# Four placements in a graph-attention kernel: inverse sums in PSUM, the last pair's order, a weight turned in row halves, count scatters among the mask's

## The reference

```python
q2 = (q @ wiq.T + biq).reshape(N, H, D).transpose(1, 0, 2)     # 16 heads of 64; k2, v2 alike
scores = jnp.einsum('hnd,hmd->hnm', q2, k2) * scale + mask[None]
attn = jax.nn.softmax(scores, axis=-1)
out = jnp.einsum('hnm,hmd->hnd', attn, v2)
out = out.transpose(1, 0, 2).reshape(N, OUT_F)
return out @ wo.T + bo
...
mask = mask.at[src, dst].set(w[edge_type - 1])     # 384 x 384, from 6144 edges
...
cnt = jax.ops.segment_sum(mask, dst, num_segments=n)     # next layer: edges per relation and target
out = out + mean @ weight[r]
```

## Time and profile before

| | us |
|---|---|
| median of 3 runs | 934.96 |
| lowest, highest run | 934.83, 941.38 |
| profiled execution | 936.0 |
| its span | 934.2 |
| TensorE busy in it | 909.6 |
| VectorE, GpSimd, ScalarE busy | 609.6, 488.5, 360.5 |

### The profile page before, as it was taken

One profiled execution on the slowest core, in us unless ns is written; L12 is line 12 of the kernel. 1 busy time (PEld: TensorE's weight loads), 2 busy tenths in 40 slices (PEclk: granted clock), 3 DMA queues, 4 the chain that ended last, 5 costly groups with the idle time before them and its releaser, 6 DMA issues.

```text
span 934.2 us, 13614 instructions
## 1 busy us (share of the span) xinstructions
PE 909.6 (97%) x4723; PEld 802.0 (86%) x4723; DVE 609.6 (65%) x1003; ACT 360.5 (39%) x568; POOL 488.5 (52%) x436
## 2 busy tenths in 40 slices
PE   4999999999999999999999999999999999999998
PEld 4999999998888887888888888888888888887886
DVE  6998888896996735655556565665656665434645
ACT  6433333344885334232323232223324345233532
POOL 5334443456686455757566575757685601320363
PEclk8999999999999999999999999999999999999999
DMA  8998755571336617454434435344333434332412
GB/s 207 239 279 224 226 159 153 152 198 1 53 52 198 166 16 269 114 155 108 154 103 159 149 112 167 94 149 113 96 107 127 158 124 139 118 105 90 137 44 91
DMA packets 89908, 128.60 MB, mean 138 GB/s; under 512 B 34481, under 2 KB 67457, under 8 KB 89857
## 3 DMA queue, kind: packets, MB, share of 16 engines
q1 hardware_dynamic: 72784, 123.54, 43.4%
q0 software_dynamic: 15552, 0.11, 4.1%
q10 hardware_dynamic: 1520, 4.30, 1.3%
HBM read 117.17 MB, written 7.59 MB: 134 GB/s over the span
## 4 chain that ended last, share of the span: by engine, by line
PE 89%; DVE 4%; ACT 2%; POOL 2%; DMA 1%; issue 1%; ACTq 0%; POOLq 0%; DVEq 0%
PE ps L671 48%; PE ps L471 17%; PE ps L745 8%; PE ps L515 4%; PE ps L634 4%; PE ps L595 2%; PE ps L551 2%; PE ps L538 1%; DMA weight_d<-weight_sum,cell 1%; PE ps L432 1%; PE ps L459 1%; DVE wlo_all L1372 1%; POOL weight_d L1865 1%; POOL mean_lo L1844 1%; PE ps L880 1%
## 5 line engine op out<-in xcount | busy, mean ns | idle before, releaser
L1372 DVE TENSOR_TENSOR wlo_all<-raw,whi_all 128x1024 fp32r<-128x1024 f32 x120 | 193.8, 1624 | 120.8 <-ACT whi_all L959 120.7
L471 PE MATMUL ps<-acts,whi_all 128*128 128x384 f32 (+1 forms) x640 | 164.2, 338 | 0.1
L1844 POOL TENSOR_TENSOR mean_lo<-mean_f,mean_hi 128x384 fp32r<-128x384 f32 x76 | 88.0, 1158 | 122.3 <-ACT mean_hi L1110 122.3
L1110 ACT ACTIVATE mean_hi<-mean_f 128x384 fp32r<-128x384 f32 x76 | 40.0, 526 | 272.7 <-DVE mean_f L1541 272.7
L671 PE MATMUL ps<-whi_all,mean_hi 128*128 128x512 f32 x452 | 139.8, 391 | 1.7 <-POOL mean_lo L1844 1.7
L671 PE MATMUL ps<-wlo_all,mean_hi 128*128 128x512 f32 x452 | 139.4, 390 | 0.0
L671 PE MATMUL ps<-whi_all,mean_lo 128*128 128x512 f32 x452 | 139.4, 390 | 0.0
L959 ACT ACTIVATE whi_all<-raw 128x1024 fp32r<-128x1024 f32 x120 | 124.6, 1049 | 23.7 <-PE ps L671 18.2
L471 PEld LDWEIGHTS ps<-acts,whi_all 128*128 128x128 f32 x640 | 116.7, 190 | 0.5 <-DVE acts L1384 0.4
L1865 POOL DMA_INDIRECT weight_d<-weight_sum,cell x48 | 95.6, 1991 | 27.6 <-DMA weight_d<-weight_sum,cell 16.7
L471 PE MATMUL ps<-acts,wlo_all 128*128 128x384 f32 (+1 forms) x320 | 107.8, 337 | 0.0
(11 more groups left out here) (209 smaller groups left out, 1723.7 us busy)
## 6 DMA issues: line engine op xcount, KB each, us to landing
raw<-in_L_gnn_weight SPq DMA_DIRECT2D x64, 512.0 KB, 3.3
rows_b<-rows_d SPq DMA_DIRECT2D x24, 384.0 KB, 5.3
raw<-in_L_gnn_w_gate SPq DMA_DIRECT2D x16, 512.0 KB, 3.3
raw<-in_L_gnn_W_self SPq DMA_DIRECT2D x16, 512.0 KB, 3.4
raw<-in_L_gnn_W_neigh SPq DMA_DIRECT2D x16, 512.0 KB, 3.8
count_d<-total_r SPq DMA_DIRECT2D x8, 576.0 KB, 5.5
rel_r<-count_d SPq DMA_DIRECT2D x8, 576.0 KB, 4.5
raw<-in_L_gnn_wq SPq DMA_DIRECT2D x32, 128.0 KB, 6.3
```

The costliest lines, as they stand in the source:

```text
L471: mm = pe.matmul(ps[:, j % 2, 0:N], stationary[j % RING][:, k, :], acts[:, a, moving, k, :], start=i == 0, stop=i == 3 * KT - 1)
L1110: act.activation(mean_of(q, k, 0)[:, 0, :], sums_of(q, k), ACT.Copy).then_inc(S["mean_hi"], 1)
L1372: dve.tensor_tensor(wlo_row[slot], raw[slot][:, :], whi_row[slot].bitcast(F32), ALU.subtract)\
L1844: pool.tensor_tensor(mean_of(q, k, 1)[:, 0, :], sums_of(q, k), mean_of(q, k, 0)[:, 0, :].bitcast(F32), ALU.subtract).then_inc(S["mean_lo"], 1)
```

## The change

Nothing is computed otherwise. Six edits:

1. `invert_sums` writes the reciprocals of heads 2 to 15 to columns 384 and on of PSUM bank 7, which `spread_sums` leaves unused, and copies them from there. It waits for `spread_read` before, and `read_spread` moves, on ScalarE, from the end of a pair to before `probs_high(o, 0)`.
2. The last pair of heads is written out on its own on TensorE, and its order on ScalarE and VectorE is changed with it; `make_pair(6)` moves behind `probs_low(o, 0)`.
3. `turn_output` turns row halves: 16 transposes of 64 rows into 64 columns each, one half in each bank; `column_high` and `column_low` read the new layout.
4. The last 16 mask scatters go in groups between the first 16 count scatters; `PAIR_AFTER` is eight counts later.
5. The 16 `meet` of the value units are spread otherwise, none in the last; the first two inversions come after the first two `probs_low`.
6. `sum_planes(0)` goes ahead of `row_parts(0)`, with a wait for `w_used`.

```diff
--- before.py
+++ after.py
@@ -196,6 +196,7 @@
         V_UNITS = NT * KT // 2
         V_COLS = 2 * P
         V_BANK = (0, 1, 6, 7)
+        ROWS = P // 2
         WO_BANK = (0, 2, 0, 2, 4, 6, 4, 6)
         T_ROOT = 7 * KT
         T_REL = T_ROOT + KT
@@ -209,7 +210,8 @@
         W_CREDIT = RING
         O_CREDIT = 2
         S_CREDIT = 2
-        PAIR_AFTER = (17, 19, 21, 25, 27, 29)
+        PAIR_AFTER = (25, 27, 29, 33, 35, 37)
+        MASK_ALONE = 2 * EC // 3
 
         FIRST = KT // 2
         TURNS = NT + KT - FIRST
@@ -456,8 +458,10 @@
                 if j > 5:
                     pe.wait_ge(S["w_lo"], T_WO + j - 1)
                 for k in range(KT):
-                    mm = pe.transpose(ps[:, WO_BANK[j] + k // 4, P * (k % 4):P * (k % 4) + P],
-                                      raw[j % RING][:, P * k:P * k + P], ident[:, :])
+                    for f in range(2):
+                        rows = slice(ROWS * f, ROWS * f + ROWS)
+                        mm = pe.transpose(ps[:, WO_BANK[j] + f, ROWS * k:ROWS * k + ROWS],
+                                          raw[j % RING][rows, P * k:P * k + P], ident[rows, rows])
                 mm.then_inc(S["weight_turned"], 1)
 
             def column_tile(g, j, a, ready=None):
@@ -601,27 +605,33 @@
                 e, o = 2 * pair, 2 * pair + 1
                 if pair and o + 1 < H:
                     scores(pair + 1, 0)
-                if o + 1 < H:
-                    scores(pair + 1, 1)
-                else:
-                    turn_output(0)
-                    turn_output(1)
+                if o + 1 == H:
+                    break
+                scores(pair + 1, 1)
                 if pair:
                     turn_probs(e, 0)
                     turn_probs(e, 1)
                     weigh_values(e - 1)
                 turn_probs(e, 2)
                 spread_sums(pair)
-                if o + 1 < H:
-                    scores(pair + 1, 2)
-                else:
-                    turn_output(2)
+                scores(pair + 1, 2)
                 turn_probs(o, 0)
                 turn_probs(o, 1)
-                if o + 1 == H:
-                    turn_output(3)
                 weigh_values(e)
                 turn_probs(o, 2)
+            turn_output(0)
+            turn_probs(H - 2, 0)
+            turn_probs(H - 2, 1)
+            spread_sums(H // 2 - 1)
+            turn_output(1)
+            weigh_values(H - 3)
+            turn_probs(H - 2, 2)
+            turn_probs(H - 1, 0)
+            turn_output(2)
+            turn_output(3)
+            turn_probs(H - 1, 1)
+            turn_probs(H - 1, 2)
+            weigh_values(H - 2)
             weigh_values(H - 1)
 
             def output_blocks(f, nt, blocks):
@@ -948,8 +958,9 @@
                 if j < RING:
                     act.wait_ge(S["w_used"], T_WO + (j + 1))
                 b = WO_BANK[j]
-                act.activation(whi[j][:, :, :] if j < RING else wo_t[0][:, j - RING, :, :],
-                               ps[:, b:b + 2, :].rearrange("p b (k n) -> p (b k) n", n=P), ACT.Copy)\
+                target = whi[j] if j < RING else wo_t[0][:, j - RING, :, :]
+                act.activation(target.rearrange("p k (f n) -> p k f n", f=2),
+                               ps[:, b:b + 2, :].rearrange("p f (k n) -> p k f n", n=ROWS), ACT.Copy)\
                    .then_inc(S["w_hi"], 1)
 
             def row_high(t, slot, use, used=None):
@@ -1057,26 +1068,27 @@
                     exp(o + 2, 0)
                 if not more:
                     column_high(0)
+                    column_high(1)
                 probs_high(e, 2)
                 if more:
                     exp(e + 2, 1)
                     exp(o + 2, 1)
-                else:
-                    column_high(1)
+                if more:
+                    read_spread(pair)
                 probs_high(o, 0)
                 if more:
                     exp(e + 2, 2)
                 else:
+                    read_spread(pair)
                     column_high(2)
                 probs_high(o, 1)
                 if more:
                     exp(o + 2, 2)
-                else:
+                probs_high(o, 2)
+                if not more:
                     column_high(3)
-                probs_high(o, 2)
                 if pair:
                     pair_high(pair - 1)
-                read_spread(pair)
 
             act.wait_ge(S["probs_turned"], H * NT)
             act.dma_start(xres[:, :, :], x.rearrange("(t p) d -> p t d", p=P)).then_inc(S["x_in"], 16)
@@ -1328,8 +1340,10 @@
                 dve.wait_ge(S["w_hi"], T_WO + (j + 1))
                 b = WO_BANK[j]
                 hi, lo = (whi[j], wlo[j]) if j < RING else [w[:, j - RING, :, :] for w in wo_t]
-                dve.tensor_tensor(lo[:, :, :], ps[:, b:b + 2, :].rearrange("p b (k n) -> p (b k) n", n=P),
-                                  hi[:, :, :].bitcast(F32), ALU.subtract).then_inc(S["w_lo"], 1)
+                dve.tensor_tensor(lo.rearrange("p k (f n) -> p k f n", f=2),
+                                  ps[:, b:b + 2, :].rearrange("p f (k n) -> p k f n", n=ROWS),
+                                  hi.rearrange("p k (f n) -> p k f n", f=2).bitcast(F32), ALU.subtract)\
+                   .then_inc(S["w_lo"], 1)
 
 
             def start_low(n):
@@ -1409,9 +1423,15 @@
             def invert_sums(o):
                 d0 = DH * (o % 2)
                 dve.wait_ge(S["exp_ready"], 6 * (o // 2) + 5 + o % 2)
-                link(dve.reciprocal(rinv[:, o % 2, :], rsum[:, o % 4, :]))
+                if o < 2:
+                    inverse = rinv[:, o, :]
+                else:
+
+                    dve.wait_ge(S["spread_read"], o // 2)
+                    inverse = ps[:, 7, N + NT * (o % 2):N + NT * (o % 2) + NT]
+                link(dve.reciprocal(inverse, rsum[:, o % 4, :]))
                 dve.tensor_copy(rinv_cols[:, o // 2 % 2, :, d0:d0 + DH],
-                                rinv[:, o % 2, :].unsqueeze(2).to_broadcast([P, NT, DH])).then_inc(S["sum_inverted"], 1)
+                                inverse.unsqueeze(2).to_broadcast([P, NT, DH])).then_inc(S["sum_inverted"], 1)
 
             def value_tiles(g):
                 met_now = g * KT * 2
@@ -1428,17 +1448,17 @@
                     if 6 <= n < 6 + NT:
                         score_max(0, n - 6)
                         score_max(1, n - 6)
-                    for n_met in range((1, 1, 2)[n % NT]):
+                    for n_met in range((2, 1, 1, 2, 1, 1, 2, 1, 1, 2, 2, 0)[n]):
                         meet(met_now)
                         met_now += 1
                     if n == V_UNITS - 2:
                         dve.wait_ge(S["w_lo"], g * KT + KT)
                         score_max(2, 0)
                         score_max(3, 0)
+                probs_low(0, 0)
+                probs_low(0, 1)
                 invert_sums(0)
                 invert_sums(1)
-                probs_low(0, 0)
-                probs_low(0, 1)
 
             for g in range(5):
                 eight_tiles(g, g + 1 if g < 3 else g - 3)
@@ -1466,25 +1486,24 @@
                     probs_low(e, 1)
                 if not more:
                     column_low(0)
-                if pair:
+                    column_low(1)
+                if pair and more:
                     make_pair(pair - 1)
                 probs_low(e, 2)
                 if more:
                     score_max(e + 2, 2)
                     score_max(o + 2, 2)
-                else:
-                    column_low(1)
                 probs_low(o, 0)
                 if more:
                     invert_sums(e + 2)
                 else:
+                    make_pair(pair - 1)
                     column_low(2)
                 probs_low(o, 1)
                 if more:
                     invert_sums(o + 2)
-                else:
-                    column_low(3)
                 probs_low(o, 2)
+            column_low(3)
 
             def last_pair_low(pair):
                 dve.wait_ge(S["pair_hi"], pair + 1)
@@ -1819,8 +1838,9 @@
 
             cells(0, 0, 0)
             pool.wait_ge(S["mask_based"], 16)
-            for c in range(EC):
+            for c in range(MASK_ALONE):
                 scatter_mask(c)
+
             def pair_low(pair):
                 pool.wait_ge(S["pair_hi"], pair + 1)
                 link(pool.tensor_tensor(o_f[:, pair, :], o_f[:, pair, :], acts[:, 0, 0, pair, :].bitcast(F32),
@@ -1829,6 +1849,9 @@
                                    None, ALU.add).then_inc(S["pair_lo"], 1)
 
             for c in range(EC):
+                if c % GROUP == 0:
+                    for m in range(MASK_ALONE + c, min(MASK_ALONE + c + GROUP, EC)):
+                        scatter_mask(m)
                 add_counts(c)
                 if c in PAIR_AFTER:
                     pair_low(PAIR_AFTER.index(c))
@@ -1874,9 +1897,10 @@
```

(5 more changed lines are left out.)

## The result

| | before | after |
|---|---|---|
| median of 8 executions each, side by side, us | 935.06 | 929.1 |
| time against before, 95% interval | | 0.9939 (0.9918 to 0.996) |
| lowest, us | 934.67 | 928.63 |
| the profiled execution, us (its span) | 936.0 (934.2) | 934.3 (932.5) |
| a second profile of the same kernel after ("again" below) | | 928.9 (927.2) |

The change gives 5.9 us where 4.6 were forecast. Six of the eight executions lie between 928.6 and 929.3, one at 931.5 and the profiled one at 934.3, so its profile shows what makes an execution long, and the second profile, of 928.9 us, what it usually does. Before, the profiled execution was also 1 us over the median.

The account below looks back on a forecast made before the run. TensorE, busy 909.6 of 934.2 us, was taken as the bound, with 5.9 us of named waits. Terms 1.6 + 0.8 + 1.9 + 0.3 = 4.6 us off the 934.96 median gave 930.4 us, range 927.5 to 934.5.

Parts of the forecast that it names:

- The fifth: Count scatters put among the mask's scatters on GpSimd: value 0.
- Inverse sums: `invert_sums` in the pair loop: copy from PSUM avoids GpSimd's hold-up; net -1.6 us, between -2.1 and 0.
- The 0.5 us set against it for `read_spread`: ScalarE's `read_spread` moved ahead of `probs_high(o, 0)` delays each of six pairs by 0.08 us; bounds nothing and 2.1 us.
- surplus of 2.1 us: Two pairs of heads cost TensorE 8.34 and 9.21 us against 7.73 undisturbed; all 2.1 us taken as gone.
- position of GpSimd's work alone: Rival: copy stalls come from GpSimd's work position, turn up elsewhere; last pair gains only 0.5 us: 933.5; chance 0.07.
- First `probs_low`: Start of attention: `turn_probs(0, 2)`'s 1.97 us wait shrinks by only 0.8 us, since `spread_sums(0)` then waits.
- Last pair: Last pair of heads, new order: 13.5 us becomes 11.6, gain 1.9 us; bounds 2.8 and 0.5 us.
- Halves: Output weight turned in row halves in `turn_output`: -0.3 us; bounds -0.9 and about +8 us.
- Count scatters: Last 16 mask scatters grouped with 16 count scatters on GpSimd; counts end some 25 us earlier; value 0.
- After 362 nothing is changed: Start of the relations: `sum_planes(0)` coming ahead gives nothing itself but keeps 4.6 us less attention from being given back.
- The mask, late: Mask lands about 209; rival: at 218, costing 3 to 4 us, 934; chance 0.1, shared with late `pair_low`.
- cover: Mask landing about 209 against TensorE's need at `scores(0, 2)`, 214.68: 5 us, each us beyond costing one.

Follow-up runs that it names:

- masks_first: Changed kernel with mask scatters all ahead of the counts', `pair_low` at its old places and relation 0's planes behind `row_parts(0)`: 936.81 us (1.0028 against before).
- before with early weights: Kernel before, with the first relation's first two weight tile loads issued ahead of SyncE's wait for the counts' last scatter: 935.5 us (1.0003).

## Why the prediction was right, and where it wasn't

The time (929.1 us against 930.4, range 927.5 to 934.5) was right, and four of the five terms were right in direction and near in size. The fifth was wrong, and the others depend on it; the time came out all the same because the edit that it priced at nothing was made with the others, and that is luck as far as the prediction goes.

- **Inverse sums, -1.6.** In the profiles -1.9 (48.49 us for six pairs became 46.63). Copy 357 ns, forecast 0.35 us. The 0.5 us set against it for `read_spread` came out at about 0.25: a pair takes 7.77 us instead of 7.73. The mechanism holds, but the step put the whole of it down to PSUM: of the surplus of 2.1 us the new places of `pair_low` alone leave 0.6 (a pair of 8.32 us), PSUM alone nothing, and PSUM on top of the places is worth 0.7 in the medians. The rival "position of GpSimd's work alone" had a part in it.
- **First `probs_low`, -0.8.** 0.9 by the trace, the 0.67 us wait at the spread included. Missing: the clock that can fall behind the 1.97 us wait, worth 1.5 us where it does. The profile of before was one where it didn't (clock 1.00 there), so its rows couldn't show it; with the edit undone in the changed kernel the medians are 1.9 us apart.
- **Last pair, -1.9.** 13.48 us became 11.39, forecast 11.6; the order alone 1.3 to 1.4.
- **Halves, -0.3.** 0.5 by the trace, 0.4 by the medians, and for the reason given: a pair of halves 0.063 us (forecast 0.07), going in and out 0.34 (forecast 0.3), so a tile alone gains 0.04 us and two in a row 0.41 (forecast nothing and 0.33), and those in the last pair nothing. The rule it was weighed against (the Trainium skill, TensorE: Matmul & The Clock Gate, section LDWEIGHTS) has a load of 128 columns cost 107 ns. Sixteen more loads with their matmuls took 0.50 us, 63 ns for two, so even side by side they are under it. The trace doesn't agree with it for loads of 64 rows.
- **Count scatters, 0.** This step failed, at "After 362 nothing is changed" and at "Value: 0". It followed GpSimd's counts and planes, and SyncE's `relation_counts(0)` from 349.14 to 325, but not what stands behind those loads in SyncE's queue: the first relation's weights, at 352.20, on ScalarE at 361.29. These set the start of the first relation (370.38). In the sum it was worth 1.4 us of wait, and without it the other terms would not have been 4.6 us but -2.2: `masks_first` takes 936.8. The prediction's own sentence, that the step is "why 4.6 us less attention isn't given back there", was right on the planes and not on the queue, and by it the edit should have been priced as what carries the rest: 7.9 us.
- **The mask, late.** Forecast: there at 209, cover until 214.7. VectorE's first use of it is at 209.25 in one profile (inverse in SBUF, load at 204.40), at 213.16 after 4.31 us of waiting in a second (again), which costs TensorE nothing, and at 216.21 in the first. So the forecast was the early end, and the cover as said. The rival's price, 3 to 4 us at a landing of 218, was too low: 2.66 us of waiting at 216.21 became 5.4 us (934.3 against 928.9) with the clock. Two of twelve executions of the changed kernel are long (931.5 and 934.3); the second was profiled and is of that kind, of the first it isn't shown.

The edits don't add up, which is why no sum of single prices gives 5.9 us. Medians, us, from three sets of runs in which before itself moved by 0.5:

| kernel | median | against after |
|---|---|---|
| after | 928.95 | |
| whole turns | 929.38 | +0.4 |
| inverse in SBUF | 929.67 | +0.7 |
| last pair as before | 930.26 | +1.3 |
| start of attention as before | 930.82 | +1.9 |
| all four undone (count edit alone) | 934.59 | +5.6 |
| count edit undone | 936.81 | +7.9 |
| all five undone (before, three sets) | 934.2 to 934.7 | +5.3 to +5.8 |

**What stays open.** Single executions 5 to 7 us above the rest turn up in kernels with the masks first too (942.05 against 936.8; before 940 to 941), where the mask isn't late; no profile caught one. And no profile of before shows the lower clock at 230 us: that part of its executions has it is argued from the two kernels that share its order there. It can't be all that spreads them: of 30 executions of before in the last set twelve took 932.9 to 933.6 us and most of the others 934.0 to 936.5, and its profiled one, at 936.0, had full clock there. So what the count edit is worth alone is known only within some 2 us either way (0.9985 to 1.0027).

## What to carry to other kernels

When a stage is made shorter, follow every queue past the next wait it meets: the next bound may be a load behind another engine's last scatter, hidden by the very time that you mean to save (here all but 1.41 us of it). Price an edit that only moves a hidden thing earlier together with the edits that uncover it, and undo it with them in place, for alone it looks like nothing (934.6) and left out it costs more than the whole change gives (936.8 against 934.6 before). Where work is placed by counting other work (`PAIR_AFTER`), a change to the other work moves it in time.

## What the runs showed of the chip

- Of four profiles with a wait of TensorE of 1.96 or 1.97 us at `turn_probs(0, 2)`, two have the lower clock behind it (clock 0.57 in 230 to 234 behind the wait that ended at 228.80 with the old start of the attention in the changed kernel, 0.50 in 230 to 232 with the count edit alone) and two don't (1.00 before, and 1.00 before with early weights). Behind 2.36, 2.66, 2.62 and 18.1 us it was each time. It then lasts 3 to 10 us, so that a short wait can cost twice itself.
- To judge by the pace, the profile's granted clock can miss it. Behind the wait for the first bias, which ends near 17.5 us and takes 2.5 to 3.7 us in all 14 profiles, TensorE does 6 to 8 instructions in 2 us (18 to 20), and 12 to 14 a little later (26 to 28). Eleven profiles give the lower level there; three, the second of the changed kernel among them, give 1.00 at the same pace. At 228 us the profile of before has the full pace too (7.73 us a pair), so its 1.00 there holds. In the changed kernel (again), windows:

```profile
18.00:20.00 2.00, 2.00 (x7) 1.99 (x7) 1.29 (x2) 0.68 (x1) 0.19 (x1) 1.00 0.24 86
...
24.00:26.00 2.00, 2.00 (x13) 2.00 (x12) 2.00 (x5) 1.54 (x2) 1.69 (x4) 1.00 0.87 336
```

- Two transposes of 64 rows issued one behind the other on different rows took 0.063 us together (0.50 / 8), one of 128 rows 0.109 us (0.87 / 8), and changing from whole to half and back 0.34 us, part of which lies ahead of the first half's record.
- VectorE and GpSimd hold each other up on SBUF both ways: a 0.29 us copy took 1.43 to 2.22 us, and GpSimd's 1.02 us addition 1.85 to 2.02 us. A copy from PSUM was never held: 14 at 357 ns, one of them in the middle of a subtraction of GpSimd's (270.36).
- A weight tile that is loaded behind four others and the counts took 9 us from its issue to its first use (352.20 to 361.29), with the DMA engines full.
